# Tail keys' values as three rounded passes, and q's high part rounded on ScalarE, in a two-layer transformer kernel

## The reference, cut to what matters

```python
# x (4, 2048, 512); ctx (4, 154, 512): 154 keys for each of 4 batches; 16 heads of 32
x = x + cross_attention_0(layernorm(x), ctx, tau, delta)
x = x + experts(layernorm(x))                  # 32 experts, the best 8 of each token
x = x + cross_attention_1(layernorm(x), ctx, tau, delta)
x = x + light(x) + heavy(the 512 best scored tokens of each batch)

# one cross_attention, each head:
scores = (q @ k.T * tau + delta) / sqrt(32)
out = softmax(scores) @ v                      # 154 keys of 32 numbers
return concat(out) @ Wo.T + bo
```

## Time and profile before

| | |
|---|---|
| median of 3 runs | 3408.61 us (3407.73 to 3411.59) |
| profiled execution, its own time | 3411.21 us |
| its span in the trace | 3409.4 us |
| busy, share of the span | PE 95%, DVE 80%, POOL 58%, ACT 47% |
| mean granted TensorE clock | 0.979 of full speed |

### The profile page before, as it was taken

The page is one execution under the profiler, slowest core; times in us unless marked ns, Lnnn a source line. Parts: engine busy times, 40 slices in busy tenths (PEclk is TensorE's granted clock), DMA queues, the critical chain, the costliest instruction groups (busy, mean ns, idle before and its releaser), DMA issues. The chain is left out here.

```text
span 3409.4 us, 55189 instructions
## 1 busy us (share of the span) xinstructions
PE 3229.7 (95%) x17324; PEld 2552.5 (75%) x17324; DVE 2731.7 (80%) x5290; ACT 1593.3 (47%) x5449; POOL 1980.0 (58%) x1823
## 2 busy tenths in 40 slices
PE   7999999999979999999999699999999969999997
PEld 5777777777648888888888577777777757678886
DVE  4788888888677878888786489999999867767775
ACT  1776767667521111111111478888888745221111
POOL 1665656656545777777776466666666633333333
PEclk8999999999979999999999899999999989999999
DMA  7345454454465676766766445555455357630111
GB/s 216 99 137 172 122 161 140 135 172 123 139 178 153 173 176 168 166 169 171 178 166 141 110 124 154 149 149 170 133 161 165 101 183 287 232 110 13 25 13 25
DMA packets 284780, 490.95 MB, mean 144 GB/s; under 512 B 54019, under 2 KB 74819, under 8 KB 283779
## 3 DMA queue, kind: packets, MB, share of 16 engines
q1 hardware_dynamic: 243698, 408.87, 39.0%
q0 software_dynamic: 32256, 77.65, 12.3%
q10 hardware_dynamic: 8592, 1.57, 0.3%
HBM read 250.32 MB, written 136.96 MB: 114 GB/s over the span
## 5 line engine op out<-in xcount | busy, mean ns | idle before, releaser
L911 ACT ACTIVATE c_pr<-ps,t_negmax 128x154 f32<-128x154 f32 x1024 | 435.5, 552 | 178.4 <-DVE t_negmax L680 176.4
L911 ACT ACTIVATE t_pr<-ps,t_negmax 128x154 f32<-128x154 f32 x1024 | 435.2, 554 | 104.5 <-DVE t_negmax L680 103.7
L608 POOL TENSOR_TENSOR c_pr<-c_pr,t_inv 128x616 f32<-128x616 f32 x256 | 317.5, 1243 | 236.7 <-DVE t_inv L695 236.3
L608 POOL TENSOR_TENSOR t_pr<-t_pr,t_inv 128x616 f32<-128x616 f32 x256 | 318.7, 1245 | 231.5 <-DVE t_inv L695 230.6
L680 DVE TENSOR_REDUCE t_negmax<-ps 128x4 f32<-128x616 f32 x512 | 403.6, 788 | 45.6 <-PE ps L976 45.2
L703 DVE COPY t_pTm<-ps 128x512 f32<-128x512 f32 x448 | 305.9, 683 | 135.2 <-PE ps L989 135.1
L976 PE MATMUL ps<-t_kst,t_stack 98*128 98x154 f32 x2048 | 352.9, 290 | 18.5 <-DMA t_stack<-t_q_low 9.5
L81 PE MATMUL ps<-e_xT_high,e_wgu_high 128*128 128x512 f32 x768 | 302.8, 394 | 1.4 <-DVE e_xT_low L1504 1.4
L976 PEld LDWEIGHTS ps<-t_kst,t_stack 98*128 98x128 f32 x2048 | 278.9, 193 | 31.6 <-issue 15.6
L83 PE MATMUL ps<-e_xT_high,e_wgu_low 128*128 128x512 f32 x768 | 300.0, 391 | 0.0
L82 PE MATMUL ps<-e_xT_low,e_wgu_high 128*128 128x512 f32 x768 | 299.7, 390 | 0.0
(11 more groups left out here) (373 smaller groups left out, 9264.5 us busy)
## 6 DMA issues: line engine op xcount, KB each, us to landing
t_stack<-t_q_high SPq DMA_DIRECT2D x1016, 64.0 KB, 2.0
c_wgu_in<-in_gate_upT SPq DMA_DIRECT2D x32, 1536.0 KB, 6.4
t_stack<-t_q_low SPq DMA_DIRECT2D x512, 64.0 KB, 2.0
x_dram<-c_wide_rows SPq DMA_DIRECT2D x32, 1024.0 KB, 7.8
c_wd_in<-in_downT SPq DMA_DIRECT2D x32, 768.0 KB, 4.6
t_xbo<-in_x SPq DMA_DIRECT2D x16, 1024.0 KB, 6.9
xw_dram<-t_z SPq DMA_DIRECT2D x16, 1024.0 KB, 5.3
t_xbo<-x_dram SPq DMA_DIRECT2D x16, 1024.0 KB, 10.7
```

Of the source, the lines that this page charges most:

```text
L608: pool.tensor_tensor(p, p, inv[:, v, :].unsqueeze(1).to_broadcast([P, KEYS, HG]), ALU.mult).then_inc(s["normed"], 1)
L911: op = act.activation(pr[:, u % 4, :, h], flat[:, col:col + KEYS], ACT.Exp, bias=negmax[:, u, h:h + 1], accum_out=total[:, u, h:h + 1])
```

## The change

- **The values' tail product.** One plain fp32 product becomes three fp32r products: high values by high softmax, high by low, low by high.
- **The softmax's tail** (`t_pTt`) is split for it. ACT's read of bank 5 now rounds to the high part (semaphore `pTt_high`), and a new DVE operation `p_tail_low` subtracts that from bank 5 and gives the low part. Only this one now signals `pTt`. It stands one slot behind ACT's: at `PT + 1`.
- **q's high part** (`query_high`) goes from DVE to ACT, at the same slots QH.
- **The tail's values** are split once for each layer, by two more DVE operations; the array in device memory has two halves: it is cleared twice as large, `store_tails` issues eight transfers in place of four, and a load fetches both halves.
- To make room, the buffer `junk2` is gone: the second stage's squares (`square`) write what nobody reads to `z` or `z_last`, with one more wait, in the last iteration. `xnT` and `oT` stand at another place in memory.

```diff
+            def p_tail_low(i, g):
+
+                dve.wait_ge(s["pTt_high"], GROUPS * i + g + 1)
+                dve.tensor_tensor(pTt[1][:], ps[0:TROWS, 5, :], pTt[0][:].bitcast(F32),
+                                  ALU.subtract).then_inc(s["pTt"], 1)
...
-                    if at == QH[0] and nxt:
-                        query_high(i + 1, 0)
-                        if not cur:
-                            query_high(0, 1)
-                    if at in QH[1:] and cur and (i, at) != (0, QH[1]):
-                        query_high(i, QH.index(at))
+                    if at - 1 in PT[:3] and cur:
+                        p_tail_low(i, PT.index(at - 1))
+                    if at - 1 == PT[3] and prev:
+                        p_tail_low(i - 1, GROUPS - 1)
...
+            def query_high(j, n):
+
+                act.wait_ge(s["q_out"], DC * j + n + 1)
...
+                act.copy(qhigh[:, n % 2, :], qT[:, n % 2, :]).then_inc(s["q_high"], 1)
...
-                act.copy(pTt[:], ps[0:TROWS, 5, :]).then_inc(s["pTt"], 1)
+                act.copy(pTt[0][:], ps[0:TROWS, 5, :]).then_inc(s["pTt_high"], 1)
...
-                pe.matmul(ps[:, B_BANK, :], vt[:, g * P:(g + 1) * P], pTt[:], start=True, stop=False,
-                          skip_group_check=True)
+                for v, p in ((0, 0), (0, 1), (1, 0)):
+                    pe.matmul(ps[:, B_BANK, :], vt[:, v, g * P:(g + 1) * P], pTt[p][:], start=(v + p == 0), stop=False,
+                              skip_group_check=True)
...
+def split_tails(dve, k, s):
+
+    high_of(dve, k["vt_parts"][:, 0, :], k["vt"][:]).then_inc(s["vt_high"], 1)
+    dve.wait_ge(s["vt_high"], 1)
+    return dve.tensor_tensor(k["vt_parts"][:, 1, :], k["vt"][:], k["vt_parts"][:, 0, :].bitcast(F32), ALU.subtract)
...
-                sp.dma_start(scr[f"vt{l}"].rearrange("b t d -> t b d"),
-                             zero[:].unsqueeze(1).to_broadcast([TROWS, B, D])).then_inc(s["cleared"], 16)
+                sp.dma_start(scr[f"vt{l}"].rearrange("w b t d -> t (w b) d"),
+                             zero[:].unsqueeze(1).to_broadcast([TROWS, 2 * B, D])).then_inc(s["cleared"], 16)
```

More of the change, by code:

```diff
@@ L133, in kv_tables @@
     k["vm"], k["vt"] = sb("vm", [P, B, D]), sb("vt", [B * KTAIL, D])
+    k["vt_parts"] = sb("vt_parts", [B * KTAIL, 2, D], F32R)
     return k
@@ L169, in store_tails @@
 def store_tails(sp, scr, l, k, s):
[L171 to L176, removed]
+    for w in range(2):
+        for h in range(HG):
+            sp.dma_start(scr[f"vt{l}"][w].rearrange("b (n h) (g e d) -> h (b n) g e d", h=HG, e=HG, d=DK)[h, :, :, h, :],
+                         k["vt_parts"][:, w].bitcast(F32).rearrange("n (g e d) -> n g e d", e=HG, d=DK)[:, :, h, :]).then_inc(
+                             s["stored"], 16)
+def split_tails(dve, k, s):
+    high_of(dve, k["vt_parts"][:, 0, :], k["vt"][:]).then_inc(s["vt_high"], 1)
+    dve.wait_ge(s["vt_high"], 1)
+    return dve.tensor_tensor(k["vt_parts"][:, 1, :], k["vt"][:], k["vt_parts"][:, 0, :].bitcast(F32), ALU.subtract)
+KV_STORED = 16 * (2 * 3 * HG + 2 + 2 * HG)
 KV_JOBS = 13
@@ L289, in _ @@
                 else:
-                    op = dve.tensor_tensor(k["vt"][:], ps[0:B * KTAIL, bank, :], k["bv"][0:B * KTAIL, :], ALU.add)
+                    dve.tensor_tensor(k["vt"][:], ps[0:B * KTAIL, bank, :], k["bv"][0:B * KTAIL, :],
+                                      ALU.add).then_inc(s["vt_out"], 1)
+                    dve.wait_ge(s["vt_out"], 1)
+                    op = split_tails(dve, k, s)
                 op.then_inc(s["evacuated"], 1)
@@ L314, in token_phase @@
         pr = c["pr"] if gate else sb("pr", [P, 4, KEYS, HG])
-        pTm, pTt = sb("pTm", [P, 2, HG, D]), sb("pTt", [TROWS, D])
+        pTm, pTt = sb("pTm", [P, 2, HG, D]), [sb(f"pTt_{part}", [TROWS, D], F32R) for part in ("high", "low")]
         negmax, total, inv = (sb(n, [P, UNITS, HG]) for n in ("negmax", "total", "inv"))
@@ L881, in square @@
                     act.wait_ge(s["ssq"], TG * j + t)
-                act.activation(junk2[:], z_of(j)[:, t, 0:D], ACT.Square,
+                if last(j) and t == 0:
+                    act.wait_ge(s["z_stored"], 16 * (NG - 1))
+                unread = z if last(j) else c["z_last"]
+                act.activation(unread[:, 0, 0:D], z_of(j)[:, t, 0:D], ACT.Square,
                                accum_out=ssq[:, t:t + 1]).then_inc(s["ssq"], 1)
@@ L931, in turn @@
                         if not cur:
+                            query_high(0, 0)
                             act.wait_ge(s["q_high"], 1)
@@ L937, in turn @@
                         query_out(i, QO.index(at))
+                    if at == QH[0] and nxt and cur:
+                        query_high(i + 1, 0)
+                    if at in QH[1:] and cur:
+                        query_high(i, QH.index(at))
                     if at in XT and nxt:
@@ L1158, in expert_slots_phase @@
         ps = c["ps"]
-        s = Sems(nc, ctx, "r", "wv_in tau_in tail scaled kf khigh matmul evacuated lowered valued stored "
+        s = Sems(nc, ctx, "r", "wv_in tau_in tail scaled kf khigh matmul evacuated lowered valued stored vt_high "
                                "made shifted exped step weights selected stepped count_mm counted0 counted1 based parted "
@@ L1270, in value_out @@
                                   ALU.add).then_inc(s["valued"], 1)
+                if n == B:
+                    dve.wait_ge(s["valued"], B + 1)
+                    split_tails(dve, k, s).then_inc(s["valued"], 1)
             logits = c["logits"][:].rearrange("p (t e) -> p t e", e=E)
```

28 lines of the change are left out of this document (13 added, 15 removed).

## The result

The changed kernel takes **3559.2 us** (median of 4 runs, 3555.64 to 3563.47) against 3410.1 us of the kernel before on the same chip: **1.0436 of it, 95% interval 1.0418 to 1.0455**, 149 us slower. The direction was forecast; the size was not: 3478 us, with a range that ended at 3518.

What follows compares the result with a forecast made beforehand. TensorE was taken as the bound, with VectorE right behind it in the second token stage. 3411.2 us profiled + 17 + 42 (stages) + 6 + 4 (phases) = 3480, about 3478 against the runs' median; range 3408 to 3518.

Steps and rivals of the forecast that it cites:

- The delays at the six places: TensorE's transposes late at first-stage groups one, two, four (+0.63, +0.15, +0.87 us) and second-stage one, three, four (+0.81, +1.84, +1.0).
- Layer norm's transposes, +0.4: First stage, first group: layer norm's low part, queued behind `p_out` on VectorE, makes its next transposes 0.4 us later.
- Each delay is taken to shift the whole row once: Both token stages: delays are not caught up, as TensorE has no idle time; net +17 and +42 us.
- third rival: Late maxima delay exponentials, these ScalarE's next tail read, while it also rounds q; 3514 to 3530 us, chance 0.14.
- The saved product: Values' tail product on TensorE: three passes for one plain product save 0.25 us a group, 32 us in all.
- q's rounding "at nothing": Four more ScalarE roundings an iteration, 2.5 us, fit into 14.4 and 9.7 us of idle time at no cost.
- VectorE's work "nothing": Token stages: four casts leave VectorE, four subtractions come; its work shrinks 0.07 to 0.15 us a group, counted as nothing.
- The first phase: First phase of keys and values: split 1.3 us, stores 2.7, larger clear and loads 2; about +6 us (3 to 8).
- The slots' phase: Second phase of keys and values: split 1.3 us plus half of 4.76 us of store issuing; about +4 us (0 to 6).
- its upper end: TensorE's saving worth nothing: +33 and +58 us for the stages, +14 for the phases, 3514 us; range reaches 3518.
- The likeliest case: Both token stages: delays at the places read, passed on as they stand; 3440 to 3505 us, chance 0.56.

Runs made afterwards that it cites:

- the maxima first: Changed kernel with the next maximum and reciprocal ahead of the subtraction, then `p_out` (statistics also ahead in the second stage's third group): 3523.6 us, 1.0335.
- A filler of the subtraction's size: Changed kernel without the new subtraction; in its place VectorE makes an equal-sized one on constants, waiting for nobody, low part left out: 3467.4 us, 1.0160.
- the passes with the split for nothing: Changed kernel without the subtraction (low part left out), q's rounding on ScalarE at other slots, clear on ScalarE's queue: 3404.4 us, 0.9981.
- the third version without a handover: Changed kernel, but ScalarE copies the tail unrounded and rounds from the copy, VectorE subtracts from copies; q retimed, clear on ScalarE's queue, second stage's last values later: 3509.1 us.

## Why the prediction was wrong

Point by point, by its own steps. Where a step is a delay at a place, it was measured so: for iterations 3 to 13 each TensorE operation's start was taken from the start of its iteration's first scores, in both kernels, and what the difference grows by at a place is that place's delay.

- **The delays at the six places: right.** First stage 0.53, 0.10 and 0.91 us (0.63, 0.15, 0.87 forecast); second stage 0.91, 1.87 and 1.18 (0.81, 1.84, 1.0). Sums 1.55 and 3.95 us an iteration against 1.65 and 3.65.
- **Layer norm's transposes, +0.4: the number right, the cause not.** They come 0.34 us later, but straight behind the scores, whose four products take 0.82 us there, as at the place shown above. Layer norm's low part ends at 558.15, when TensorE is still at the scores, so the 0.34 belong to the next point (the two waits fall together here).

```profile
557.47 0.99 PE L1002 MATMUL ps<-t_kst,t_stack 98*128 98x154 f32 x4
558.29 0.61 PE L987 MATMUL ps<-ident,c_x_turn 128*128 128x128 f32 x4
...
557.49 0.66 DVE L727 TENSOR_TENSOR t_xnT_low<-ps,t_xnT_high 128x512 fp32r<-128x512 f32 x1
```

- **"Each delay is taken to shift the whole row once": the step that failed.** A late maximum delays the exponential, and through the bank that two units' scores share TensorE is stopped a second time, 0.25 to 0.34 us behind three late places of each stage: 0.9 and 1.0 us an iteration, 30 us in all. A further 0.75 us an iteration, 12 us, are stopped in the second stage at the place where ScalarE and not the maximum was late. The sum of 42 us agrees with the scores' waits, 40. The forecast named the late maximum as queued behind the wait and gave it no price; its third rival had late exponentials and a ScalarE that also rounds q, but its 3514 to 3530 were too low. Showing run: the maxima first, -36 us, with the reservations made there.
- **The saved product: mis-sized.** 0.16 us a group and not 0.25, since the last pass is followed 0.33 us later: 128 x 0.09 = 12 us less.
- **q's rounding "at nothing": wrong as placed.** 20 us when it alone is moved, none at other slots. Idle time of an engine in sum was taken for cover; the second rounding stands just ahead of ScalarE's tail read of the last group, and q comes late to the stack. That the place costs it is shown. By which way is open: from 140 to 900 us of that run TensorE's products wait 5.0 us at the scores with no releaser shown (1.5 before) and 4.4 at the transposes for GpSimd's multiplications (0.9), and none of it is put down to the tail read. In the kernel after it can't be added as it stands: the scores that come 0.30 and 0.51 us late in that run come 0.11 late or not at all there.
- **VectorE's work "nothing": mis-sized.** A filler of the subtraction's size, somewhat dearer than it, costs 33 us, though four casts of about the same length were taken off. The total was balanced; the place, ahead of `p_out` and the maximum, was not.
- **The first phase: +11.7 for +6.** Not the split, but the larger clear, taken as 2 us. SP's rows, the first key stores before and then the phase after:

```profile
21.13 2.13 SPq L160 DMA_DIRECT2D kst_dram<-kv_k_high  x2
23.30 1.91 SPq L160 DMA_DIRECT2D kst_dram<-kv_k_low  x1
25.25 3.42 SPq L160 DMA_DIRECT2D kst_dram<-kv_k_high  x2
```

```profile
11.56 6.92 SPq L241 DMA_DIRECT2D vt_dram<-kv_zero  x2
21.60 6.31 SPq L161 DMA_DIRECT2D kst_dram<-kv_k_high  x2
27.95 2.52 SPq L161 DMA_DIRECT2D kst_dram<-kv_k_low  x1
30.52 5.82 SPq L161 DMA_DIRECT2D kst_dram<-kv_k_high  x2
...
55.64 4.85 SPq L174 DMA_DIRECT2D vt_dram<-kv_vt_parts  x8
```

The tail's eight stores take 2.1 us more (2.7 forecast). The clear itself ends its issuing before the keys are ready; but the key stores behind it on the same queue take 6.3, 2.5 and 5.8 us to issue in place of 2.1, 1.9 and 3.4, and with the clear on another queue the 7 us are gone.
- **The slots' phase: -1 for +4.** The split and the further stores are covered there; -1.1 is just under the lower end of 0.

Missing were 33 us in the first stage and 43 in the second. By place, in the kernel after: the first stage's iteration grows by 2.9 us, 1.55 at the places and 0.9 at the scores, less 0.65 from the passes. The 1.0 us left is in smaller pieces; the largest, 0.5 us, is a wait of the transposes near the iteration's start for `p_out`, which the run with the filler has too and those without a subtraction have not. The second stage's iteration grows by 5.6 us: 3.95 at the places and 1.7 at the scores, less 0.65; the rest, 0.6, is the balance of the clock's falls and smaller pieces. So the second stops explain about 42 of the 76 us and the passes 12; what the rest divides into is not shown.

The range failed mainly because its upper end was built by taking away the saving, not by pricing what the late maximum does to the engine that sets the time. The likeliest case came out with the sign right and not quite half the size, because the chain was followed up to the first engine that was late, and not round the loop to that engine's next wait.

## What to carry to other kernels

When a wait is put into an engine's row, follow each operation queued behind it to its consumer, and that consumer's output back to the bounding engine, until the loop closes: here the second loop (exponential, shared bank, scores) cost some 40 us beside 88 us of delays at the places themselves. An engine's idle share says how much work fits in a stage, not at which slot; in the kernel before the same four roundings cost 20 us at one set of slots and nothing at another. Before splitting an operand for cheaper passes, run the passes with the split for nothing: here that gave 6 us.

## What the runs showed of the hardware

In the kernel after the subtraction with one operand in PSUM took 657 to 693 ns in all of its 128 instances, 62 of them beside a GpSimd operation; with both operands in SBUF, in the third version without a handover, it took 658 to 1789 ns. The 28 instances there that overlap no GpSimd operation took 0.68 us, all of them; the others went up to 1.79. The Trainium skill, SBUF — State Buffer, section "SBUF: two separate sides", has VectorE with two SBUF operands and a GpSimd operation that reads SBUF lock one pair of ports for a whole instruction, and the other wait; these runs agree. So in that version an early copy out of PSUM, meant to free a bank, made the later work dearer.
